# A two-layer convolution kernel: widening in float32, four buffers of node values in place of three, and group sums from one pair matrix and the identity

## The chip, the core and the metric

The kernel runs on one core of one Trainium2 chip. The metric is the device time in microseconds (us) of one execution. A core has five engines that run side by side and meet through semaphores: TensorE (PE in the profile; its weight loads are PEld), VectorE (DVE), ScalarE (ACT), GpSimd (POOL) and SyncE (SP), which here only starts transfers. TensorE writes to PSUM, eight banks of 2 KB in each of 128 partitions.

## The reference

```
x: (32, 64, 112, 112) float32
layer 0:  x = x + conv3x3(groupnorm32(x), sign(w) * alpha)          # 64 -> 64 channels
layer 1:  n = groupnorm32(x)
          h = w_in @ n                                              # 64 -> 256 channels
          h = irfft2(rfft2(8x8 patches of h) * fft_filt)
          h = depthwise conv3x3(h, w_dw)
          g = gelu(h[:128]) * h[128:]
          x = x + w_out @ g                                         # 128 -> 64 channels
```

groupnorm32 has 32 groups, so a group is two neighbouring channels.

## The kernel before

Two batch images lie on the 128 partitions (2 x 64 channels); there are 16 such pairs, which the code calls images n, and each is cut into 14 strips of 8 rows. A strip is 14 patches of 8x8 pixels, or 7 blocks of two patches; the blocks are worked in four groups, 0 to 2 of two blocks (512 columns of PSUM, 256 channels each) and 3 of one block (256 columns).

A strip of layer 1 goes through: normalising (ScalarE, L456), transposition to pixels on partitions (TensorE, L921), the copy xT (ScalarE, L464), the forward transform into an orthonormal basis of the patch's frequencies (TensorE, L930), and its copy xf (ScalarE, L469), which lies in the same memory as xT. xf is then split into two float16 halves, xf_hi (ScalarE, L478) and xf_lo (GpSimd, L351). *Widening* (`widened`, TensorE, L941) multiplies with w_in, split likewise into win_hi and win_lo: four products of halves, accumulated in PSUM, for each block and each of the two batch images. VectorE multiplies with the filter (`filtered`, hf, L690). *Evaluation* (`evaluated`, TensorE, L953, float32) takes the values of the patch at 121 nodes of a Toom-Cook scheme; VectorE multiplies them with the depthwise taps at the nodes (`weighted`, v32, L697). The products are split again: v_hi (ScalarE, L487) and v_lo (GpSimd, `low_nodes`, L357). *Interpolation* (`interpolated`, TensorE, L971) gives the 10x10 extended patches; then come gelu (ScalarE), the gate g (VectorE, L722), carries between strips (L706, L713, L511, L516), the projection with w_out (TensorE, L985) and the residual (GpSimd, L364).

The order of the work is written out by hand for every engine, step by step. In step t the front (transposition and transform) works on strip t, `mid` (widening, evaluation, v) on strip t-1, `up` (interpolation, gate) on strip t-2 and `done` (projection, residual) on strip t-3. Each image has 14 steps. Layer 0 of the *next* image runs in between: its statistics in steps 0 to 4, its group sums in step 5, and in steps 6 to 12 two convolution strips each (L912); the group sums of the next layer 1 stand in step 13. I call steps 6 to 12 convolution steps and the others plain; their orders differ. The last image has plain steps only.

PSUM banks 0-1 (P) and 2-3 (Q) are used in turn by widening, evaluation, transposition, transform and convolution. v32 has three buffers; the table V_BUF says which group of which image goes where, and VectorE waits, before each `weighted`, until GpSimd has read the buffer's last content (semaphores pool_vlo). In a plain step the order of v products is image 0: groups 3, 2, 1, 0; image 1: groups 3, 0, 1, 2. GpSimd's order in a plain step is v_lo of (0,3), residual, v_lo of (0,2), (0,1), (0,0), (1,3), then xf_lo, then v_lo of (1,0), (1,1), (1,2), residual.

Group sums (`groups`, L887 and L888): a pair matrix with 0.5 in 2x2 blocks gives the group's mean and mean variance, and a matrix c_apart = identity - pair gives each channel's distance from the group mean, whose square VectorE adds to the variance.

Of the kernel before, what the change touches and what calls it, by code (L numbers as in the profile page):

```python
# [10 lines left out]
P = 8  # L11
C = 64
# [59 lines left out]
def shape_constants():  # L72
# [18 lines left out]
    return {"forward": np.concatenate([basis, basis]), "pick": pick, "pair": pair, "apart": np.eye(HC) - pair, "identity": np.eye(HC),  # L91
# [3 lines left out]
def build(nc, x, conv_w, alpha, w_in, w_dw, filt, w_out, forward, pick, pair, apart, identity, nodes, taps, ext, out):  # L95
# [37 lines left out]
    with ctx:  # L133
# [8 lines left out]
        c_apart = sb("c_apart", [128, 128])  # L142
# [4 lines left out]
        win_hi = sb("win_hi", [128, C2], F16)  # L147
        win_lo = sb("win_lo", [128, C2], F16)
# [12 lines left out]
        xf_hi = sb("xf_hi", [128, NBLK, BPX], F16)  # L161
        xf_lo = sb("xf_lo", [128, NBLK, BPX], F16)
        hf = sb("hf", [BPX, IMGS, NBLK, C2])
        v32 = sb("v32", [128, 3, 2, 2, C2])
# [23 lines left out]
        win_sb = v32[:, 2, 0, 0, :]  # L188
# [39 lines left out]
        pool_xl = sem("pool_xl")  # L228
        act_xh = sem("act_xh")
# [18 lines left out]
        N_CONST = 15  # L248
# [34 lines left out]
        def _(sp):  # L283
# [10 lines left out]
            for dst, src in ((c_fwd[:], forward), (c_pick, pick), (c_pair[:], pair), (c_apart[:], apart), (c_id[:], identity),  # L294
                             (c_nodes[:], nodes), (c_taps, taps), (ext32, ext), (filt_sb, filt), (wdw_sb, w_dw),
                             (wout_sb[:], w_out), (win_sb[0:C], w_in), (win_sb[C:128], w_in)):
                sp.dma_start(dst, src).then_inc(dma_const, 16)
# [31 lines left out]
        def _(pool):  # L329
# [19 lines left out]
            def spectrum_low(n, s):  # L349
                pool.wait_ge(act_xh, n * STRIPS + s + 1)  # L350
                nc.gpsimd.tensor_tensor(xf_lo[:], xf[:], xf_hi[:], ALU.subtract).then_inc(pool_xl, 1)  # L351

            def low_nodes(b, s, img, grp):
# [3 lines left out]
                nc.gpsimd.tensor_tensor(v_lo[:, img, :, k0:k1, :], v32[:, V_BUF[kind(b, s)][img][grp], :, 0:k1 - k0, :],  # L357
# [9 lines left out]
            def image(n, par, prev, front, more):  # L367
                for t in range(STRIPS if front else OUT):
                    mid = item(n, t, MID, prev, front)
                    done = item(n, t, OUT, prev, front)  # L370
                    if more and CONV_FROM <= t <= CONV_TO:
# [14 lines left out]
                        if front:  # L386
                            spectrum_low(n, t)
# [5 lines left out]
                    else:  # L393
# [15 lines left out]
                        if front:  # L409
                            spectrum_low(n, t)  # L410
# [20 lines left out]
        def _(act):  # L431
# [41 lines left out]
            def spectrum_high(n, s):  # L473
# [781 lines left out]
```

## Time and profile before

| | |
|---|---|
| time, median of 3 runs | 5405.63 us (5405.21 to 5406.29) |
| profiled execution | 5406.3 us, span 5404.5 us |
| PE busy | 5202.6 us (96%) |
| PEld busy | 3195.1 us (59%) |
| DVE busy | 4642.3 us (86%) |
| ACT busy | 3739.5 us (69%) |
| POOL busy | 4643.1 us (86%) |
| granted TensorE clock | 0.996 of full speed |

The span is the time from the first to the last event of the profiled execution. Busy is the time in which an engine has at least one instruction under way; matmuls overlap each other, so the time from one start to the next says more of TensorE's pace than the length of one. L numbers are lines of the kernel before. A float32 matmul stands in the trace as two instructions.

### The profile page before, as it was taken

To read this page: it belongs to the slowest core of one execution; us is meant where nothing else is said; L and a number is where in the kernel's file an instruction comes from. 1 tells how busy PE (TensorE), PEld (TensorE's weight loads), DVE (VectorE), ACT (ScalarE), POOL (GpSimd) and SP (SyncE) were. 2 spreads that over 40 slices of the span, in tenths; PEclk is the share of its full clock that TensorE was granted. 3 is DMA by queue.
4 is the path that set the end of the run, shared out by engine and by line. 5 is a ranking of instruction groups with operands and counts; after the bars stand their busy time and mean duration, and the time that the engine had idled before them with its cause. 6 is when DMAs were issued, how large, how long until landed. Compare 5 with 4: busy or idle time off the path is not lost.

```text
span 5404.5 us, 201429 instructions
## 1 busy us (share of the span) xinstructions
PE 5202.6 (96%) x88868; PEld 3195.1 (59%) x88868; DVE 4642.3 (86%) x5703; ACT 3739.5 (69%) x4866; POOL 4643.1 (86%) x2727
## 2 busy tenths in 40 slices
PE   5999999999999999999999999999999999999998
PEld 4565655656556565565656556565665655656554
DVE  6889888888888888888898888988889888888876
ACT  3766767677676766767767676676766767677675
POOL 3889889898888988889888898888989889898898
PEclk9999999999999999999999999999999999999999
DMA  2011110110101111010010101101011110110000
GB/s 103 19 50 42 38 44 29 53 40 37 54 22 50 40 40 53 19 57 36 36 53 32 48 33 39 54 36 43 33 50 40 40 42 31 50 43 20 23 26 26
DMA packets 43953, 219.31 MB, mean 41 GB/s; under 512 B 5366, under 2 KB 6104, under 8 KB 36952
## 3 DMA queue, kind: packets, MB, share of 16 engines
q1 hardware_dynamic: 43096, 206.42, 9.9%
q8 instruction: 716, 11.73, 0.9%
q14 instruction: 141, 1.16, 0.1%
HBM read 103.64 MB, written 102.76 MB: 38 GB/s over the span
## 4 chain that ended last, share of the span: by engine, by line
PE 69%; DVE 15%; POOL 7%; issue 5%; ACT 3%; DMA 0%; DVEq 0%; SPq 0%; POOLq 0%; ACTq 0%
PE PS L953 20%; PE PS L971 17%; PE PS L912 14%; PE PS L941 10%; POOL v_lo L357 6%; DVE v L697 5%; PE PS L985 5%; DVE hf L690 4%; DVE g L722 2%; PE PS L921 2%; ACT v_hi L487 2%; DVE bn L628 2%; DVE PS L713 1%; ACT carry L516 1%; POOL xf_lo L351 0%
## 5 line engine op out<-in xcount | busy, mean ns | idle before, releaser
L357 POOL TENSOR_TENSOR v_lo<-v,v_hi 128x1024 f16<-128x1024 f32 (+1 forms) x1792 | 3354.6, 1898 | 455.4 <-ACT v_hi L487 455.0
L697 DVE TENSOR_TENSOR v<-PS,smul 128x1024 f32<-128x1024 f32 (+1 forms) x1792 | 1910.4, 1086 | 361.6 <-POOL v_lo L357 200.9
L487 ACT ACTIVATE v_hi<-v 128x1024 f16<-128x1024 f32 (+1 forms) x1792 | 1646.8, 944 | 717.5 <-DVE v L697 561.9
L953 PE MATMUL PS<-hf,c_nodes 64*64 64x512 f32 (+1 forms) x14336 | 1659.7, 556 | 70.4 <-DVE v L697 57.0
L971 PEld LDWEIGHTS PS<-c_ext,v_hi 128*128 128x128 f16 x14336 | 1129.9, 97 | 507.2 <-ACT carry L511 165.0
L971 PE MATMUL PS<-c_ext,v_hi 128*128 128x100 f16 (+2 forms) x14336 | 1258.9, 203 | 9.7 <-issue 4.1
L971 PE MATMUL PS<-c_ext,v_lo 128*128 128x100 f16 (+2 forms) x14336 | 1250.6, 202 | 0.0
L971 PEld LDWEIGHTS PS<-c_ext,v_lo 128*128 128x128 f16 x14336 | 1118.2, 97 | 1.2
L690 DVE TENSOR_TENSOR hf<-PS,mult 128x1024 f32<-128x1024 f32 (+1 forms) x896 | 954.8, 1086 | 86.7 <-PE PS L941 66.2
L953 PEld LDWEIGHTS PS<-hf,c_nodes 64*64 64x64 f32 x14336 | 406.8, 131 | 623.1 <-DVE v L697 219.7
L912 PE MATMUL PS<-S_hi,csign 64*64 64x448 f16 (+2 forms) x8640 | 746.8, 336 | 9.4 <-POOL S_lo L346 9.4
L912 PE MATMUL PS<-S_lo,csign 64*64 64x448 f16 (+2 forms) x8640 | 748.0, 337 | 0.0
L464 ACT ACTIVATE xT<-PS 128x896 f32<-128x896 f32 x224 | 205.6, 918 | 638.9 <-PE PS L921 638.9
L722 DVE TENSOR_TENSOR g<-PS,gel 128x912 f32<-128x912 f32 (+1 forms) x448 | 496.3, 1108 | 58.7 <-DVE PS L713 2.0
L346 POOL TENSOR_TENSOR S_lo<-n,S_hi 128x896 f16<-128x896 f32 x224 | 411.0, 1835 | 150.7 <-ACT S_hi L448 150.7
L351 POOL TENSOR_TENSOR xf_lo<-xT,xf_hi 128x896 f16<-128x896 f32 x224 | 425.5, 1900 | 83.4 <-ACT xf_hi L478 83.4
L941 PE MATMUL PS<-win_hi,xf_hi 64*128 64x256 f16 x3136 | 435.8, 274 | 59.0 <-DVE hf L690 33.1
L507 ACT ACTIVATE gel<-PS 128x912 f32<-128x912 f32 (+1 forms) x448 | 413.5, 923 | 110.1 <-DVE PS L706 109.0
L985 PE MATMUL PS<-g,wout_sb 128*64 128x448 f32 (+2 forms) x1792 | 445.6, 574 | 4.0 <-DVE g L722 2.3
L941 PE MATMUL PS<-win_hi,xf_lo 64*128 64x256 f16 x3136 | 429.1, 270 | 0.0
L941 PE MATMUL PS<-win_lo,xf_hi 64*128 64x256 f16 x3136 | 429.1, 270 | 0.0
L941 PE MATMUL PS<-win_lo,xf_lo 64*128 64x256 f16 x3136 | 429.0, 269 | 0.0
(74 smaller groups left out, 5846.0 us busy)
## 6 DMA issues: line engine op xcount, KB each, us to landing
out_x<-Xa SPq DMA_DIRECT2D x96, 448.0 KB, 2.5
out_x<-Xb SPq DMA_DIRECT2D x96, 448.0 KB, 2.5
Xa<-in_x SPq DMA_DIRECT2D x8, 2240.0 KB, 9.0
Xb<-in_x SPq DMA_DIRECT2D x8, 2240.0 KB, 8.9
Xa<-in_x SPq DMA_DIRECT2D x8, 1792.0 KB, 7.7
Xb<-in_x SPq DMA_DIRECT2D x8, 1792.0 KB, 6.8
Xa<-in_x SPq DMA_DIRECT2D x8, 1344.0 KB, 5.9
Xb<-in_x SPq DMA_DIRECT2D x8, 1344.0 KB, 6.7
```

Source lines behind the costliest of these rows:

```text
L351: nc.gpsimd.tensor_tensor(xf_lo[:], xf[:], xf_hi[:], ALU.subtract).then_inc(pool_xl, 1)
L357: nc.gpsimd.tensor_tensor(v_lo[:, img, :, k0:k1, :], v32[:, V_BUF[kind(b, s)][img][grp], :, 0:k1 - k0, :], v_hi[:, img, :, k0:k1, :], ALU. ...
L487: nc.scalar.activation(v_hi[:, img, :, k0:k1, :], v32[:, V_BUF[kind(b, s)][img][grp], :, 0:k1 - k0, :], ACT.Copy).then_inc(act_vhi[img], 1)
L507: nc.scalar.activation(gel[:, :, r0:r1, :], Y[:, :, r0:r1, :], ACT.Gelu).then_inc(act_y0, 1)
L690: nc.vector.tensor_tensor(hf[:, :, k0:k1, :], PS[:, bank:bank + 2, 0:(k1 - k0) * C2].rearrange("p i (k c) -> p i k c", c=C2), mult[:].unsq ...
L697: nc.vector.tensor_tensor(v32[:, V_BUF[kind(b, s)][img][grp], :, 0:k1 - k0, :], PS[:, bank:bank + 2, 0:(k1 - k0) * C2].rearrange("p i (k c ...
L722: nc.vector.tensor_tensor(g[:, img, r0:r1, :].rearrange("p r (b c) -> p b r c", c=YC), Y[:, :, r0:r1, :], gel[:, :, r0:r1, :], ALU.mult).t ...
L912: last = nc.tensor.matmul(PS[c * C:(c + 1) * C, bank + h, i0 * W:(i0 + m) * W], csign[r * C:(r + 1) * C, tap, :], S[r * C:(r + 1) * C, row ...
L941: last = nc.tensor.matmul(PS[:, bank + r, (k - k0) * C2:(k - k0 + 1) * C2], xf[r * C:(r + 1) * C, k, :], win[r * C:(r + 1) * C, :], start= ...
L953: last = nc.tensor.matmul(PS[points, bank + side, 0:(k1 - k0) * C2], c_nodes[half, points], hf[half, img, k0:k1, :].rearrange("p k c -> p ...
L971: last = nc.tensor.matmul(Y[:, b0, :, col - b0 * YC:end - b0 * YC], v[:, img, patch % 2, patch // 2, half * HC:(half + 1) * HC], c_ext[:, ...
L985: last = nc.tensor.matmul(Z[img * C:(img + 1) * C, 0:(r1 - r0) * HALF_W], wout_sb[:], g[:, img, r0:r1, 1 + q * HALF_W:1 + (q + 1) * HALF_W ...
```

## The change

Widening is done in float32: TensorE takes xf and w_in as they are, in four matmuls a block, one for each 64x64 tile (batch image r, side of the block), and nothing is accumulated. xf_hi, xf_lo, win_hi, win_lo and the instructions that made them go; w_in gets memory of its own. ScalarE's copy of the next pixels into xT, which waited for GpSimd's xf_lo, waits for the last widening of the strip before. v32 gets a fourth buffer, and a product's buffer is its place in the order of its image; V_BUF goes. The product at place k of image 1 waits for GpSimd's v_lo at place k of image 0 of the same strip, and that of image 0 for image 1's of the strip before. The pair matrix is passed with its sign turned, c_apart goes, and its product is made by two accumulated matmuls, identity and then pair; three signs in VectorE's small operations follow.

```diff
-    return {"forward": ..., "pair": pair, "apart": np.eye(HC) - pair, "identity": np.eye(HC),
+    return {"forward": ..., "pair": -pair, "identity": np.eye(HC),
...
-    V_BUF = {"plain": [{3: 0, 2: 1, 1: 2, 0: 0}, {3: 1, 0: 2, 1: 0, 2: 1}],
-             "conv": [{3: 0, 0: 1, 1: 2, 2: 0}, {3: 1, 2: 2, 1: 0, 0: 1}]}
...
-        v32 = sb("v32", [128, 3, 2, 2, C2])
+        v32 = sb("v32", [128, 4, 2, 2, C2])
...
 # ScalarE: pixels
                 if n or s:
-                    act.wait_ge(pool_xl, n * STRIPS + s)
+                    act.wait_ge(pe_hf, 4 * (n * STRIPS + s))
...
 # ScalarE: spectrum_high and GpSimd: spectrum_low, in every step
-                nc.scalar.activation(xf_hi[:], xf[:], ACT.Copy).then_inc(act_xh, 1)
-                nc.gpsimd.tensor_tensor(xf_lo[:], xf[:], xf_hi[:], ALU.subtract).then_inc(pool_xl, 1)
...
 # VectorE, plain step (before = not the very first strip)
                         if mid:
-                            if before and conv_before:
-                                dve.wait_ge(pool_vlo[1], 4 * i - 1)
-                            elif before:
-                                dve.wait_ge(pool_vlo[1], 4 * i - 1)
+                            if before:
+                                dve.wait_ge(pool_vlo[1], 4 * i - 3)
                             weighted(b, s, 0, 3, BANK_P)
...
                         if mid:
-                            dve.wait_ge(pool_vlo[0], 4 * i + 2)
+                            dve.wait_ge(pool_vlo[0], 4 * i + 1)
                             weighted(b, s, 1, 3, BANK_Q)
...
                         if mid:
-                            dve.wait_ge(pool_vlo[0], 4 * i + 3)
+                            dve.wait_ge(pool_vlo[0], 4 * i + 2)
                             weighted(b, s, 1, 0, BANK_Q)
...
 # TensorE
-                return nc.tensor.matmul(Z[:, 2:3], c_apart[:], channels[:, 0:1], start=True, stop=True)
+                nc.tensor.matmul(Z[:, 2:3], c_id[:], channels[:, 0:1], start=True, stop=False)
+                return nc.tensor.matmul(Z[:, 2:3], c_pair[:], channels[:, 0:1], start=False, stop=True)
...
             def widened(b, s, grp, bank):
-                pe.wait_ge(pool_xl, b * STRIPS + s + 1)
+                pe.wait_ge(act_xf, b * STRIPS + s + 1)
                 for k in range(k0, k1):
-                    for part, (xf, win) in enumerate(((xf_hi, win_hi), (xf_lo, win_hi), (xf_hi, win_lo), (xf_lo, win_lo))):
-                        for r in range(IMGS):
-                            last = nc.tensor.matmul(PS[:, bank + r, (k - k0) * C2:(k - k0 + 1) * C2],
-                                                    xf[r * C:(r + 1) * C, k, :], win[r * C:(r + 1) * C, :],
-                                                    start=part == 0, stop=part == 3)
+                    for r, side in ((0, 0), (1, 1), (0, 1), (1, 0)):
+                        last = nc.tensor.matmul(PS[side * P * P:(side + 1) * P * P, bank + r, (k - k0) * C2:(k - k0 + 1) * C2],
+                                                xf[r * C:(r + 1) * C, k, side * P * P:(side + 1) * P * P],
+                                                win_sb[r * C:(r + 1) * C, :], start=True, stop=True)
                 last.then_inc(pe_hf, 1)
```

The order on TensorE in step 5 of the first image, before: the end of one widening call, the group sums (L887, L888) and the start of the next call.

```order
L941 MATMUL PS<-win_hi,xf_hi 128x256 x2
L941 MATMUL PS<-win_hi,xf_lo 128x256 x2
L941 MATMUL PS<-win_lo,xf_hi 128x256 x2
L941 MATMUL PS<-win_lo,xf_lo 128x256 x2
L887 MATMUL PS<-mvx,c_pair 128x2
L888 MATMUL PS<-mvx,c_apart 128x1
L941 MATMUL PS<-win_hi,xf_hi 128x256 x2
```

The same place after (here three widening calls of 20 matmuls read as one row, and each tile has 64 rows):

```order
L931 MATMUL PS<-c_ext,v_hi 128x10x10
L901 MATMUL PS<-win_sb,xT 64x256 x20
L847 MATMUL PS<-mvx,c_pair 128x2
L848 MATMUL PS<-mvx,c_id 128x1
L849 MATMUL PS<-mvx,c_pair 128x1
L901 MATMUL PS<-win_sb,xT 64x256 x8
L931 MATMUL PS<-c_ext,v_hi 128x10x10
```

A block has four matmul calls in place of eight, and the group sums three in place of two; no call has moved past another.

The order on GpSimd in a plain step of the first image, before (Xa is the residual, v_lo in 128x2x256 is group 3):

```order
L357 TENSOR_TENSOR v_lo<-v,v_hi 128x2x256
L364 TENSOR_TENSOR Xa<-g,Xa 128x8x56
L357 TENSOR_TENSOR v_lo<-v,v_hi 128x2x512 x3
L357 TENSOR_TENSOR v_lo<-v,v_hi 128x2x256
L351 TENSOR_TENSOR xf_lo<-xT,xf_hi 128x896
L357 TENSOR_TENSOR v_lo<-v,v_hi 128x2x512 x3
```

And after:

```order
L343 TENSOR_TENSOR v_lo<-v,v_hi 128x2x256
L350 TENSOR_TENSOR Xa<-g,Xa 128x8x56
L343 TENSOR_TENSOR v_lo<-v,v_hi 128x2x512 x3
L343 TENSOR_TENSOR v_lo<-v,v_hi 128x2x256
L343 TENSOR_TENSOR v_lo<-v,v_hi 128x2x512 x3
```

Only xf_lo is gone from between the products of image 1. VectorE's order of operations is the same as before in every step; only the numbers it waits for have changed.

## Rows read from the trace of the kernel before

**Rows 1.** Windows: us; busy PE, PEld, DVE, ACT, POOL; clock; DMA. Statistics, convolution, plain.
```profile
2154.66:2175.45 20.79, 19.73 (x322) 11.70 (x320) 19.24 (x25) 14.72 (x20) 18.75 (x12) 1.00 0.06 21
...
2226.52:2253.08 26.56, 26.45 (x477) 16.52 (x476) 22.77 (x28) 18.72 (x24) 22.73 (x14) 1.00 0.05 19
...
5241.90:5262.48 20.58, 19.66 (x322) 11.71 (x320) 16.20 (x19) 14.86 (x20) 18.80 (x12) 1.00 0.07 25
```

**Rows 2.** Timeline, TensorE: start, us, instruction; convolution step, then plain step.
```profile
2228.70 0.66 PE L953 MATMUL PS<-hf,c_nodes 64*64 64x256 f32 x8
2229.18 0.99 PE L930 MATMUL PS<-c_fwd,xT 64*64 64x64 f32 x56
2230.25 1.09 PE L953 MATMUL PS<-hf,c_nodes 64*64 64x512 f32 x8
...
5184.56 0.66 PE L953 MATMUL PS<-hf,c_nodes 64*64 64x256 f32 x8
...
5186.57 1.09 PE L953 MATMUL PS<-hf,c_nodes 64*64 64x512 f32 x8 [0.54 <-DVE v L697]
```

**Rows 3.** Timeline, VectorE: the same convolution step and plain step.
```profile
2229.50 0.69 DVE L697 TENSOR_TENSOR v<-PS,smul 128x512 f32<-128x512 f32 x1 [0.29 <-PE PS L953]
...
5185.82 0.69 DVE L697 TENSOR_TENSOR v<-PS,smul 128x512 f32<-128x512 f32 x1 [0.76 <-POOL v_lo L357]
```

**Rows 4.** Timeline, GpSimd: the same plain step.
```profile
5183.64 7.47 POOL L357 TENSOR_TENSOR v_lo<-v,v_hi 128x1024 f16<-128x1024 f32 x4 [1.43 <-ACT v_hi L487]
5191.08 1.90 POOL L351 TENSOR_TENSOR xf_lo<-xT,xf_hi 128x896 f16<-128x896 f32 x1
```

**Rows 5.** Waits of the span: who for whom, us in total, times, longest.
```profile
DVE v L697 <- POOL v_lo L357: 200.9, 328, 1.4
...
PE PS L953 <- DVE v L697: 57.0, 107, 1.8
```

**Rows 6.** Chain of waits at the start: start, us, what.
```profile
37.27 0.43 DVE win_lo L865
...
110.81 0.96 ACT xf_hi L478
...
111.83 1.89 POOL xf_lo L351
```

**Rows 7.** Timeline, TensorE: widening calls in the plain step.
```profile
5193.61 0.27 PE L941 MATMUL PS<-win_hi,xf_hi 64*128 64x256 f16 x2
...
5194.57 0.28 PE L941 MATMUL PS<-win_hi,xf_hi 64*128 64x256 f16 x2
...
5196.00 0.28 PE L941 MATMUL PS<-win_hi,xf_hi 64*128 64x256 f16 x2 [0.38 <-DVE hf L690]
```

**Rows 8.** Timeline, TensorE: another convolution step.
```profile
2004.86 1.09 PE L953 MATMUL PS<-hf,c_nodes 64*64 64x512 f32 x8
2005.88 0.22 PE L971 MATMUL PS<-c_ext,v_hi 128*128 128x100 f16 x1
...
2007.37 1.95 PE L953 MATMUL PS<-hf,c_nodes 64*64 64x512 f32 x16
2009.25 0.99 PE L985 MATMUL PS<-g,wout_sb 128*64 128x448 f32 x4
2010.21 0.28 PE L941 MATMUL PS<-win_hi,xf_hi 64*128 64x256 f16 x2
...
2011.19 0.22 PE L971 MATMUL PS<-c_ext,v_hi 128*128 128x100 f16 x1
```

**Rows 9.** Line L930 over the span: duration min/median/max in ns.
```profile
L930 PEld LDWEIGHTS PS<-c_fwd,xT x12544: 129/135/228, 108.0 to 5350.9; 64*64 64x64 f32 x200
L930 PE MATMUL PS<-c_fwd,xT x12544: 216/218/366, 108.0 to 5351.0; 64*64 64x64 f32 x200
```

**Rows 10.** Timeline, TensorE: group sums in step 5.
```profile
2190.82 0.38 PE L887 MATMUL PS<-mvx,c_pair 128*128 128x2 f32 x2
2191.07 0.36 PE L888 MATMUL PS<-mvx,c_apart 128*128 128x1 f32 x2
```

More of the change, by code:

```diff
@@ L90, in shape_constants, with build @@
     pair = np.kron(np.eye(HC // 2), np.full((2, 2), 0.5))
-    return {"forward": np.concatenate([basis, basis]), "pick": pick, "pair": pair, "apart": np.eye(HC) - pair, "identity": np.eye(HC),
+    return {"forward": np.concatenate([basis, basis]), "pick": pick, "pair": -pair, "identity": np.eye(HC),
             "nodes": np.concatenate([nodes, nodes]), "taps": taps, "ext": ext}
-def build(nc, x, conv_w, alpha, w_in, w_dw, filt, w_out, forward, pick, pair, apart, identity, nodes, taps, ext, out):
+def build(nc, x, conv_w, alpha, w_in, w_dw, filt, w_out, forward, pick, pair, identity, nodes, taps, ext, out):
     B, _, H, W = x.shape
@@ L293, in _ @@
                 sp.dma_start(alpha_sb[r * C:(r + 1) * C], alpha).then_inc(dma_conv, 16)
-            for dst, src in ((c_fwd[:], forward), (c_pick, pick), (c_pair[:], pair), (c_apart[:], apart), (c_id[:], identity),
+            for dst, src in ((c_fwd[:], forward), (c_pick, pick), (c_pair[:], pair), (c_id[:], identity),
                              (c_nodes[:], nodes), (c_taps, taps), (ext32, ext), (filt_sb, filt), (wdw_sb, w_dw),
-                             (wout_sb[:], w_out), (win_sb[0:C], w_in), (win_sb[C:128], w_in)):
+                             (wout_sb[:], w_out), (win_sb[0:C, :], w_in), (win_sb[C:128, :], w_in)):
                 sp.dma_start(dst, src).then_inc(dma_const, 16)
@@ L356, in low_nodes @@
                 pool.wait_ge(act_vhi[img], 4 * (b * STRIPS + s) + at + 1)
-                nc.gpsimd.tensor_tensor(v_lo[:, img, :, k0:k1, :], v32[:, V_BUF[kind(b, s)][img][grp], :, 0:k1 - k0, :],
+                nc.gpsimd.tensor_tensor(v_lo[:, img, :, k0:k1, :], v32[:, V_ORDER[kind(b, s)][img].index(grp), :, 0:k1 - k0, :],
                                         v_hi[:, img, :, k0:k1, :], ALU.subtract).then_inc(pool_vlo[img], 1)
@@ L486, in high_nodes @@
                     act.wait_ge(pe_y, 4 * i - 2 + 2 * img)
[L487 removed]
+                nc.scalar.activation(v_hi[:, img, :, k0:k1, :], v32[:, V_ORDER[kind(b, s)][img].index(grp), :, 0:k1 - k0, :],
                                      ACT.Copy).then_inc(act_vhi[img], 1)
@@ L697, in weighted @@
                 nc.vector.tensor_tensor(
-                    v32[:, V_BUF[kind(b, s)][img][grp], :, 0:k1 - k0, :],
+                    v32[:, V_ORDER[kind(b, s)][img].index(grp), :, 0:k1 - k0, :],
                     PS[:, bank:bank + 2, 0:(k1 - k0) * C2].rearrange("p i (k c) -> p i k c", c=C2),
@@ L762, in image @@
                         if mid:
-                            dve.wait_ge(pool_vlo[0], 4 * i + 1)
+                            if before:
+                                dve.wait_ge(pool_vlo[1], 4 * i)
                             weighted(b, s, 0, 2, BANK_P)
@@ L806, in image @@
                         if mid:
[L807 to L810 removed]
+                            if before:
+                                dve.wait_ge(pool_vlo[1], 4 * i - 3)
                             weighted(b, s, 0, 3, BANK_P)
[L812 to L815 removed]
+                            if before:
+                                dve.wait_ge(pool_vlo[1], 4 * i - 2)
                             weighted(b, s, 0, 2, BANK_Q)
@@ L821, in image @@
                         if mid:
-                            if before and conv_before:
-                                dve.wait_ge(pool_vlo[1], 4 * i - 2)
-                            elif before:
-                                dve.wait_ge(pool_vlo[1], 4 * i - 2)
+                            if before:
+                                dve.wait_ge(pool_vlo[1], 4 * i - 1)
                             weighted(b, s, 0, 1, BANK_Q)
-                            dve.wait_ge(pool_vlo[0], 4 * i + 1)
+                            if before:
+                                dve.wait_ge(pool_vlo[1], 4 * i)
                             weighted(b, s, 0, 0, BANK_P)
```

72 lines of the change are left out of this document (18 added, 54 removed).

## The prediction

> **What bounds the kernel now.** The busy shares of the whole span come first, but three engines are above 80% there, and that does not say which of them ends a wait. So I cut the span at the starts of successive strip transposes and read the windows [rows 1]. The reader is to see that there are only two kinds of step. A step with convolutions takes 26.56 us of which TensorE is busy 26.45: nothing but TensorE's own time counts there. A plain step takes about 20.6 us with 19.66 on TensorE, 16.2 on VectorE (19.24 where it also takes statistics) and 18.8 on GpSimd. There are 7 convolution steps in each of 15 images, 105, and 7 x 15 + 14 = 119 plain ones.
>
> Next I looked for the missing 0.9 us of a plain step, in the timelines. With x2 or x8 in a row several instructions are merged. TensorE evaluates the 256-wide group of the second image (E3), runs the forward transform (F), and then must wait with the next evaluation until VectorE has emptied the bank of E3. From E3 to that next evaluation the plain step takes 5186.57 - 5184.56 = 2.01 us, the convolution step 2230.25 - 2228.70 = 1.55 [rows 2]. On VectorE the reason is plain: its v product starts 5185.82 - 5184.56 = 1.26 us after E3 in the plain step, released by GpSimd's v_lo, and 0.80 us after E3 in the convolution step, released by TensorE [rows 3]. v32 has three buffers, and GpSimd holds the one wanted. GpSimd works from 5183.64 without a pause: four v_lo (7.47 us), then xf_lo (1.90 us) before the v_lo of the next groups [rows 4]. Over the span TensorE idles 57.0 us in 107 places for a v product, while VectorE waits 200.9 us in 328 places for v_lo, most of it with no consequence [rows 5].
>
> **The v32 buffers.** With four buffers, buffer = place in the order, the product of (image 1, group 3) waits for v_lo of (image 0, group 3) in place of that of (image 0, group 2). The former is done by 5182.2, where GpSimd begins to idle 1.43 us, the latter, the first of the four, by 5185.8 [rows 3, 4]. So the product is free to go as soon as E3 has ended and VectorE is idle. E3 ends at 5185.22 (start 5184.56, took 0.66) and VectorE is free from 5185.82 - 0.76 = 5185.06 [rows 2, 3]: start near 5185.3, as in the convolution step. The later products wait for one v_lo less in the same way. Nothing new is queued behind them. TensorE gets back, in each of the 107 places, 57.0 / 107 = 0.53 us less the 0.07 that stays even in the convolution step (F runs 2229.18 + 0.99 = 2230.17, the evaluation starts at 2230.25 [rows 2]). That is 57.0 - 107 x 0.07 = 49.5. One place, the longest (1.8 us), lies in the tail, where GpSimd's chain ends last anyway: 48 us back. Bounds: nothing, if another wait stands behind it; 57 if all goes.
>
> What is late next in a plain step with statistics is VectorE: 19.24 busy [rows 1] plus some 20 hand-overs. Its statistics sit right behind the waiting product and move up with it, so it starts its own long stretch some 0.5 earlier, and the gain should survive. Below it lies TensorE's 19.66.
>
> **The halves of the spectrum go.** ScalarE loses xf_hi (0.96 us a step) and GpSimd xf_lo (1.90) [rows 4, 6]. Each is hidden already in the steady state: widening is a step later. I price them at nothing there, beside giving GpSimd 1.9 us of slack a step, with which v_lo of the last groups comes 1.9 earlier. They are on the chain only in the first image, where TensorE waits for xf_hi 0.96 and xf_lo 1.89 before its first widening, and then in its second step again for xf_lo [rows 6]: the first 0.96 + 1.89 = 2.9 us, and of the 1.9 of the second I take 1.5, since TensorE still has an interpolation to end: 4.4 us gained. ScalarE's wait for the pixels moves from xf_lo to the last widening of the step before; TensorE issues all four widenings ahead of the transposes that ScalarE waits for anyway, so it is free.
>
> **The widening itself.** Before: for each of 7 blocks, 8 float16 matmuls of 256 columns, two at a time (the two row halves). After: 8 instructions of float32 on four 64x64 tiles at a time (each float32 matmul is two instructions: F has 56 [rows 2] where the code makes 7 x 4). A two-block call before takes 0.96 to the next call (5193.61 to 5194.57) and 0.98 to an interpolation (2010.21 to 2011.19); a block's 8 rows are some 0.44 [rows 7, 8]. For float32 the same shape is in the trace: E3 is one block of 256 columns. From its start to F is 0.48 (2228.70 to 2229.18 [rows 2]). A 512-column evaluation: two of them and the gap to the next line are 2009.25 - 2007.37 = 1.88 us, 0.43 for each round of four beyond the first and about 0.05 once at a call's start [rows 8]. So 256 columns take 0.215 a round, two rounds a block, 0.43: the same as before. A two-block call is 0.05 + 4 x 0.215 = 0.91 against 0.96, before an interpolation 1.02 (2004.86 to 2005.88) against 0.98, the one-block call 0.48 against 0.44 [rows 2, 7, 8].
>
> That rounds with a new stationary side each time run that fast is shown by F: 56 instructions, 14 rounds, in 0.99 - 0.22 = 0.77 for 13 intervals, 0.059 a round of 64 columns, with 8 weight loads a block [rows 2, 9]. The Trainium skill (TensorE: Matmul & The Clock Gate, The mechanism) says that a weight load overlaps running matmuls only when its row group differs. By that rule each round of four, which occupies both row groups, would bare its load; F's 0.059 a round, with loads of 135 ns each [rows 9], disagrees, so I keep it as the basis of a rival below.
>
> In a plain step the second-last widening call is followed by a wait for VectorE (5194.57 to 5196.00, 1.43 us [rows 7]), which swallows the 0.05 saved in the two-block calls, while the 0.04 of the one-block call and 0.04 of the last call move the chain of hf products: +0.07 a step, 119 x 0.07 = 8.3 us. In a convolution step the call before the interpolation costs 0.04 more, and the next three, which VectorE's hf products pace, -0.01 and +0.03 (the longer last round, before whose end VectorE may not start): +0.06, 105 x 0.06 = 6.3 us. Bounds from the same rows: if each of the three two-block calls saves its 0.05 and nothing swallows it, 224 x 0.15 = -34 us; if each of the four calls costs 0.04 more with no cover, 224 x 0.16 = +36 us.
>
> **Group sums.** One matmul more, two instructions, in 2 x 16 places. In the step of the statistics they stand between widening calls; the first line takes 0.25 (2190.82 to 2191.07 [rows 10]), and the new one adds as much. The two that stand there now fill the wait for VectorE (1.43 us after the call's start, less its own 0.96, leaves 0.47 [rows 7]), so little covers the third: 0.2 x 30 = 6 us, and nothing for the two before the first strip. The sign folded into the matrix changes no instruction's size. The two casts of w_in leave VectorE at the start (0.43 us on the chain for one [rows 6], 0.6 for both), and one 64 KB load of a constant goes: 0.6 us.
>
> **Sum.** -48 - 4.4 - 0.6 + 8.3 + 6.3 + 6 = -32.4 us. The execution profiled took 5406.3 us (span 5404.5 and 1.8 around it), 0.7 above the median of 5405.63. 5406.3 - 32.4 = 5373.9; from the median it would be 5373.2. I say 5374.
>
> **Rivals.**
> First, slower. The float32 rounds do not hide their weight loads. Place: every widening, 14 rounds a step of which 4 open a call. Price: the 0.05 us that a call's first round already pays, for the other 10: 0.5 us x 224 = 112 us, so 5374 + 112 less some cover in the plain steps, about 5475. It decides from 32.4 / 224 = 0.14 us a step, 14 ns for each of the 10 rounds. For it: a stationary side that is data with 256 moving columns stands nowhere in the trace. Against: F. The skill's rule above would give this result.
> Second, the gain meets a new wait. In the steps with statistics (3 of 7 plain ones, 45 in all, with the 0.47 wait) VectorE, at 19.24 of 20.79 us [rows 1], has no room and holds the step: 45 x 0.47 = 21 us less gain, 5395. For it: that share. Against: its stretch starts when the product does.
> Third, more is gained. GpSimd's slack and ScalarE's 0.95 us also loosen hand-overs that I count as fixed (the 0.07 at each of the 107 places, 7.5 us), and the widening's 14.6 are covered: 5374 - 7.5 - 14.6 = 5352.
> That the change does nothing of what it says (the wait only changes its name, 5400) I hold for nearly excluded, since the convolution step shows the place without the GpSimd wait.
>
> **Chances.** Forecast 0.72 (5364 to 5386), slower rival 0.06, statistics 0.12, more gained 0.10. A measurement of this kernel tells 0.2%, 11 us, from no change; faster than 5394.8 is the forecast, the third rival and a third of the second with it, 0.86; the same 0.08; slower 0.06. The range that holds 8 in 10 runs from 5356 to 5393: the low end some way to the third rival, the high end nearly to the second and to half of the +36 of the widening.
>
> **What would show it.** Plain steps of about 20.2 us in place of 20.6, convolution steps at 26.6; TensorE's wait for v products from 57 to below 12 us; VectorE's wait for v_lo near zero; GpSimd near 78% busy (18.8 - 1.9 in a plain step); a two-block widening call at 0.91 us, its rounds 0.215 apart. Wrong would be rounds of 0.26 or more, convolution steps of 27 us or more (first rival), or statistics steps that stay at 20.7 while the last image's fall (second).

## The result and the profile after

| | time, median | ratio to before, 95% interval |
|---|---|---|
| before, 20 runs | 5405.1 us | |
| changed, 20 runs | 5396.25 us (5393.1 to 5398.88) | 0.9983 [0.9977, 0.9990] |

The change saves 8.9 us, 0.17%, and the interval lies clear of 1. 5374 was forecast, with 5356 to 5393 as the range, so the gain is about a quarter of the 32 us forecast.

First the page of the changed kernel: the span, then the busy time of each engine.

```profile
span 5394.6 us, 200882 instructions
PE 5249.1 (97%) x88932; PEld 3061.1 (57%) x88932; DVE 4631.7 (86%) x5701; ACT 3526.7 (65%) x4642; POOL 4236.2 (79%) x2503
```

GpSimd is at 79% (78% was expected) and ScalarE lost 4 points. But TensorE has 46.5 us *more* busy time than before (5202.6). Next the windows from one strip transpose to the next, in the order of [rows 1]: a step with statistics, a convolution step, a plain step of the last image, and, fourth, step 13.

```profile
2148.28:2168.58 20.30, 19.89 (x322) 11.08 (x320) 19.31 (x25) 13.77 (x19) 16.91 (x11) 1.00 0.05 21
2219.23:2245.95 26.72, 26.61 (x477) 15.89 (x475) 22.68 (x28) 17.76 (x23) 20.74 (x13) 1.00 0.05 20
5235.13:5255.38 20.25, 19.84 (x322) 11.07 (x320) 16.25 (x19) 13.91 (x19) 16.94 (x11) 1.00 0.06 24
...
2399.07:2419.70 20.63, 19.94 (x321) 11.08 (x319) 19.84 (x24) 13.92 (x19) 16.84 (x11) 1.00 0.07 25
```

The statistics step fell from 20.79 to 20.30 and the plain one from 20.58 to 20.25; the convolution step rose from 26.56 to 26.72. The medians over images 1 to 14, from the starts of the transposes, in us:

| step | 0 | 1 | 2 | 3 | 4 | 5 | 6 to 11 each | 12 | 13 | sum |
|---|---|---|---|---|---|---|---|---|---|---|
| before | 20.70 | 20.39 | 20.16 | 20.79 | 20.66 | 30.41 | 26.56 | 18.10 | 20.70 | 331.3 |
| after | 20.30 | 20.53 | 20.05 | 20.30 | 20.60 | 30.05 | 26.72 | 18.49 | 20.62 | 331.3 |

A row of the table runs from the transpose of that step to the next, so the group sums of steps 5 and 13 fall into columns 4 and 12. The fourteen middle images gain nothing. What is gained lies in the first image (328.6 to 323.2), the last one (267.5 to 264.1 for 13 steps) and the tail. The steps without convolutions are also less alike than the prediction's two kinds had them: in the kernel before, TensorE's wait for a v product is 0.5 to 0.6 us in steps 0, 3, 4, 5 and 13, 0.27 in step 2, and none in step 1.

The waits (engine, line, released by: us in total, times, longest) say that the wait in question is gone, and which one grew:

```profile
DVE v L670 <- POOL v_lo L343: 5.5, 17, 0.6
PE PS L913 <- DVE v L670: 4.5, 12, 0.9
...
PEld PS L901 <- DVE hf L663: 160.5, 312, 0.8
DVE hf L663 <- PE PS L901: 101.0, 322, 3.9
```

Against [rows 5], VectorE's wait for v_lo fell from 200.9 us to 5.5 and TensorE's for a v product from 57.0 to 4.5. In their place the two engines wait for each other at widening. Before, these two rows were:

```profile
PEld PS L941 <- DVE hf L690: 103.9, 296, 0.7
...
DVE hf L690 <- PE PS L941: 66.2, 185, 6.7
```

TensorE in the plain step shows both. E3, F and the next evaluation, which answer to [rows 2]:

```profile
5199.00 0.66 PE L913 MATMUL PS<-hf,c_nodes 64*64 64x256 f32 x8
5199.48 0.99 PE L891 MATMUL PS<-c_fwd,xT 64*64 64x64 f32 x56
5200.55 1.09 PE L913 MATMUL PS<-hf,c_nodes 64*64 64x512 f32 x8
```

5200.55 - 5199.00 = 1.55 us where it was 2.01. And widening, which answers to [rows 7] (the first row is three calls merged, the second the last call):

```profile
5207.14 2.57 PE L901 MATMUL PS<-win_sb,xT 64*64 64x256 f32 x40
5210.05 1.09 PE L901 MATMUL PS<-win_sb,xT 64*64 64x256 f32 x16 [0.34 <-DVE hf L663]
5211.07 0.22 PE L931 MATMUL PS<-c_ext,v_hi 128*128 128x100 f16 x1
```

From the first call to the last are 2.91 us, before 5216.59 - 5213.76 = 2.83 in the last image; the last call takes 1.02 to the interpolation, before 0.98.

### The profile page after: what moved, and what is told of

Its sections match the earlier page's. It is cut to its first block, busy times and chain, and to the rows that moved or that the text cites. A ratio compares the mean times of both kernels' runs of the same rounds, so it can differ in the third digit from the quotient of the medians.

```text
span 5394.6 us, 200882 instructions
## 1 busy us (share of the span) xinstructions
PE 5249.1 (97%) x88932; PEld 3061.1 (57%) x88932; DVE 4631.7 (86%) x5701; ACT 3526.7 (65%) x4642; POOL 4236.2 (79%) x2503
## 2 busy tenths in 40 slices
DMA packets 43804, 219.20 MB, mean 41 GB/s; under 512 B 5350, under 2 KB 5960, under 8 KB 36808
## 4 chain that ended last, share of the span: by engine, by line
PE 86%; DVE 10%; issue 3%; DMA 0%; ACT 0%; POOL 0%; DVEq 0%; SPq 0%; POOLq 0%; ACTq 0%
PE PS L913 28%; PE PS L931 21%; PE PS L873 14%; PE PS L901 12%; PE PS L945 7%; DVE v L670 5%; PE PS L882 4%; DVE hf L663 3%; DVE bn L601 1%; DVE g L695 1%; DVE PS L679 0%; DVE PS L686 0%; DMA alpha_sb<-in_alpha 0%; POOL v_lo L343 0%; PE PS L847 0%
## 5 line engine op out<-in xcount | busy, mean ns | idle before, releaser
L901 PE MATMUL PS<-win_sb,xT 64*64 64x256 f32 x12544 | 824.9, 388 | 48.0 <-DVE hf L663 28.9
L901 PEld LDWEIGHTS PS<-win_sb,xT 64*64 64x64 f32 x12544 | 413.7, 132 | 394.3 <-DVE hf L663 160.5
L945 PE MATMUL PS<-g,wout_sb 128*64 128x448 f32 (+2 forms) x1792 | 445.6, 574 | 7.7 <-DVE g L695 5.9
L873 PEld LDWEIGHTS PS<-S_hi,csign 64*64 64x64 f16 x8640 | 314.1, 107 | 142.8 <-DVE v L670 28.5
L873 PEld LDWEIGHTS PS<-S_lo,csign 64*64 64x64 f16 x8640 | 314.6, 106 | 135.2 <-issue 32.1
L469 ACT ACTIVATE g<-PS 128x448 f32<-128x448 f32 (+1 forms) x448 | 244.7, 546 | 81.3 <-PE PS L945 79.3
```

The source lines that it names most:

```text
L873: last = nc.tensor.matmul(PS[c * C:(c + 1) * C, bank + h, i0 * W:(i0 + m) * W], csign[r * C:(r + 1) * C, tap, :], S[r * C:(r + 1) * C, row ...
L901: last = nc.tensor.matmul(PS[side * P * P:(side + 1) * P * P, bank + r, (k - k0) * C2:(k - k0 + 1) * C2], xf[r * C:(r + 1) * C, k, side * ...
L945: last = nc.tensor.matmul(Z[img * C:(img + 1) * C, 0:(r1 - r0) * HALF_W], wout_sb[:], g[:, img, r0:r1, 1 + q * HALF_W:1 + (q + 1) * HALF_W ...
```

## The experiments

Ratios are to the kernel before, run beside each. "Plain" is a step of the last image, "conv" a convolution step, before 20.57 and 26.56.

The forecasts name their theories by a letter. A and B are one pair in experiments 1 and 4, and others in 2 and in 3.

### 1 to 4: one part at a time

**1.** Before, with four places for node values. To fit, one is of half size and xf_lo lies over xf; widening stays in float16.

```diff
-        xf_lo = sb("xf_lo", [128, NBLK, BPX], F16)
+        xf_lo = xT[...].bitcast(F16)...
+        v3 = sb("v3", [128, 2, 1, C2])
-                    act.wait_ge(pool_xl, n * STRIPS + s)
+                    act.wait_ge(pe_hf, 4 * (n * STRIPS + s))
```

> The kernel before with a fourth v32 buffer alone (the place of group 3, always first, is half as wide, and xf_lo lies in the memory of xT, so that it fits; ScalarE's next pixels then wait for the last widening). Widening stays in float16, group sums as before. Theory A (the buffers give all that was predicted, and the loss lies in the float32 widening and the group sums): the wait for the v product after the forward transform falls from 1.53 to 1.06 us in plain steps, 46 us less in all, about 5359. Theory B (the buffers' gain is itself given back in a later wait, whatever the widening): 5385 to 5400.

5397.08 us, 0.9984 [0.9976, 0.9993]; plain 20.52, conv 26.56. That is theory B. The wait for the buffer is gone, and most of the gain with it. The waits of this kernel (L933 is widening, xT now also holds xf_lo, L945 evaluation) and a piece of its chain:

```profile
PE PS L933 <- POOL xT L353: 50.6, 81, 4.0
...
PE PS L945 <- DVE v L699: 5.3, 12, 0.9
```
```profile
5200.15 7.47 POOL v_lo L359 x4
5207.62 1.86 POOL xT L353
5209.48 0.14 issue
5209.62 0.63 PE PS L933 x8
```

GpSimd's order did not move when TensorE came earlier: four v_lo, then xf_lo, and widening now stands waiting for it. In step 3 of the middle images the evaluation behind F starts 0.56 us earlier than before, the first widening only 0.06. In the kernel before, xf_lo ended at 5191.08 + 1.90 = 5192.98 [rows 4], and the first widening of that step stands here:

```profile
5193.17 0.28 PE L941 MATMUL PS<-win_hi,xf_hi 64*128 64x256 f16 x2
```

It was early by 0.19 us, and the chain above has 0.14 from the end of xf_lo to the widening that waited for it, so that some 0.05 was to spare. In steps 2 and 5 of the middle images it was 0.15 already before the change: nothing to spare. The 50.6 us of this wait must not be set against the 51.7 won for v products: 22.0 of them lie in step 5, which keeps its length (30.42) and where the kernel before waited too, 1.24 us a time under the name of a v product, and 8.3 in the first image. The plain steps proper hold 20.

**2.** Before, with widening in float32 alone (three buffers, old group sums).

> The kernel before with the float32 widening alone (no xf_hi, xf_lo, win_hi, win_lo), three v32 buffers, old group sums. Theory A (each of the four widening calls of a step costs TensorE 0.04 more, since its first weight load stands bare behind a semaphore wait and a float32 load is longer): 224 x 0.15 = +34, less 4.4 at the start, about 5435. Theory B (the widening is as cheap as forecast, +10): 5415. The v product's wait stays at 1.53 us in plain steps in both, since it hangs on v_lo of the same strip that stands ahead of xf_lo in GpSimd's order.

5434.41 us, 1.0049 [1.0035, 1.0063]; plain 20.72, conv 26.72. The time is theory A's; its cause is not, as experiments 7 to 11 show. A convolution step costs 0.16 us more (0.06 was forecast), a plain step of the last image 0.14 (0.07 was forecast). In the middle images the medians of steps 0, 2, 3, 5 and 13 rise by 0.06 to 0.10 only, of step 1 by 0.13 and of step 4 by 0.19. The wait for the buffer stays.

**3.** Before, with the new group sums alone.

> The kernel before with the new group sums alone (pair matrix and identity, one matmul more, in 30 places of the loop). Theory A: 0.22 us of TensorE each, +6 to +7, about 5412. Theory B (covered by the wait for VectorE's product): within 1 us of before.

5415.18 us, 1.0018 [1.0009, 1.0027]; 5412 was forecast by theory A, and B is out. The two steps with group sums take 0.23 us more. In the changed kernel:

```profile
2183.61 0.38 PE L847 MATMUL PS<-mvx,c_pair 128*128 128x2 f32 x2
2183.86 0.36 PE L848 MATMUL PS<-mvx,c_id 128*128 128x1 f32 x2
2184.08 0.36 PE L849 MATMUL PS<-mvx,c_pair 128*128 128x1 f32 x2
2184.37 1.09 PE L901 MATMUL PS<-win_sb,xT 64*64 64x256 f32 x16
```

**4.** Parts 1 and 3 together: the changed kernel but for the float32.

> The changed kernel with the widening put back into float16 halves (four v32 buffers and the new group sums stay; xf_lo in the memory of xT). Theory A: e1 plus the group sums, 5359 + 7 = 5366, that is 30 below the changed kernel. Theory B (something other than the widening eats the gain): above 5385.

5403.74 us, 0.9998 [0.9989, 1.0007]. Theory B holds, and the changed kernel is 7.5 us faster than this one: float32 costs TensorE time, but gives back a little more by taking xf_lo off GpSimd.

### 5 and 6: the same buffers with xf_lo earlier

```diff
                             low_nodes(mid[0], mid[1], 0, 0)
-                            low_nodes(mid[0], mid[1], 1, 3)
                         if front:
                             spectrum_low(n, t)
                         if mid:
+                            low_nodes(mid[0], mid[1], 1, 3)
                             low_nodes(mid[0], mid[1], 1, 0)
```

> The kernel before, widening in float16, with the four places for node values of the first experiment (one of half size, xf_lo written over xf), and one thing moved: in a step without convolution GpSimd makes xf_lo ahead of the low half of image 0's last group, v_lo(1,3), not behind it. Theory C: the gain of the four places is real (0.41 us a plain step from transform to evaluation) and was taken back in the first experiment because xf_lo came 0.41 us late for widening; made some 1.16 us earlier it is no longer late, and a plain step is 20.57 - 0.41 = 20.1 to 20.2 us in place of 20.52: 119 x 0.41 = 49 less than before, 5355 to 5362 us, and the first weights of widening wait for VectorE's hf again. Rival D (the buffers alone are worth no more than 8 us in any order, the waits lie elsewhere, or v_lo(1,3), now 1.9 us later, holds image 1): over 5385 us.

5372.71 us, 0.9939 [0.9927, 0.9952], 33 us less than before. Windows of steps 3 and 5 and of the plain step:

```profile
2142.34:2162.57 20.23, 19.73 (x321) 11.71 (x319) 19.31 (x25) 14.71 (x20) 18.75 (x12) 1.00 0.06 23
2182.77:2213.40 30.63, 28.98 (x482) 17.21 (x480) 24.40 (x29) 23.72 (x31) 29.70 (x19) 1.00 0.08 32
...
5192.69:5212.80 20.11, 19.66 (x322) 11.73 (x320) 16.26 (x19) 14.87 (x20) 18.75 (x12) 1.00 0.06 24
```

Theory C stands: the plain step is 20.11, 0.46 less, and step 3, with statistics, fell by 0.56. The memory is laid out as in experiment 1, so that it was the order and not the layout that ate the gain there. C's 5355 to 5362 was too low: it counted 0.41 in all 119 steps. Step 1 (20.39) had no wait for a v product and gains nothing, step 2 gains 0.27, and there are two places more. Step 5 rose from 30.41 to 30.61: GpSimd is busy 29.70 of it, and the chain there is GpSimd alone up to the convolution (L904):

```profile
2194.76 3.22 POOL v_lo L359 x2
2197.98 1.79 POOL S_lo L348
2199.77 4.21 POOL v_lo L359 x2
2203.98 1.79 POOL S_lo L348
2205.77 1.02 POOL Xa L366
2206.80 1.12 POOL v_lo L359
2207.91 1.80 POOL S_lo L348
...
2209.84 3.62 PE PS L904 x72
```

The changed kernel, without xf_lo, runs that step in 30.05. The other place is step 13 (20.56), below.

**6.** The same with fewer waits and the distance from the group mean made by VectorE:

```diff
-                nc.tensor.matmul(Z[:, 2:3], c_id[:], channels[:, 0:1], ...)
-                return nc.tensor.matmul(Z[:, 2:3], c_pair[:], channels[:, 0:1], ...)
+                nc.vector.tensor_tensor(groupx[:, 2:3], mvx[:, 0:1], Z[:, 0:1], ALU.add)
```

> As the kernel with xf_lo made earlier, and three things more: the wait for xf_lo stands at the first widening call of a step alone, the second call's implied wait for VectorE is gone, and a group's distance from its mean is made by VectorE from the mean of the pair matrix (no identity product). If a wait at the head of a call costs its bare first load some 0.01 us in float16, 1 to 3 us less than that kernel; group sums as before or 3 us less. Theory C: 5350 to 5362. Theory D: over 5385.

5371.09 us, 0.9937 [0.9924, 0.9949], within 2 us of the fifth, where 5350 to 5362 was forecast. The column with the group sums of layer 0 fell from 20.19 to 20.11; the plain step did not move, and step 5 rose from 30.61 to 30.70.

### 7 to 11: why float32 costs 0.15 us a step

My theory was that each wait at the head of a call bares the first float32 weight load. In the changed kernel most calls do start with 0.267 us from the first to the second round of four, against 0.216 later.

```diff
# 7
-                pe.wait_ge(act_xf, b * STRIPS + s + 1)
                 for k in range(k0, k1):
+                    pe.wait_ge(act_xf, b * STRIPS + s + 1)
# 8
-                pe.wait_ge(act_xf, b * STRIPS + s + 1)
+                if first:
+                    pe.wait_ge(act_xf, b * STRIPS + s + 1)
```

> The changed kernel with one thing added: the wait for xf, long met, stands ahead of each block of a widening call and not ahead of the call alone (3 more waits a step, 672 in all). Theory (the first weight load behind a wait lies bare, in float32 0.05 us of it): 672 x 0.05 = 34 us slower, 5430. Rival (a met wait costs nothing; the four calls are longer by their streams or by the gap to what follows): 5396, within 3 us.

> The changed kernel with the wait for xf at the first widening call of a step alone, and without the implied wait for VectorE ahead of the second call of a step without convolution; calls two to four keep a wait for VectorE wherever their bank has a reader before them. Theory (a wait bares the first float32 load): only a call left with no wait gains, one of four in plain steps, 119 x 0.05 = 6 us, 5390 us. Rival: 5396, within 3 us.

With more waits 5395.07 us, 0.9982 [0.9973, 0.9991]; with fewer 5401.75, 0.9993 [0.9984, 1.0002]. The theory falls: 672 waits more cost nothing, and with fewer nothing is won. The round behind an added wait stays at 0.216 us, where a bared load would have made it 0.267; in both kernels plain is 20.25, conv 26.72 and each call as long as in the changed kernel. The eighth is 5.5 us above the changed kernel, though the intervals of the two ratios overlap (0.9984 to 1.0002 and 0.9977 to 0.9990). Its profile shows single steps that are 0.3 us or more over their median, 11.1 us in the middle images against 5.7; why, stays open.

The next theory (L) looked at who waits for the end of a call. The times from the start of one call to the next in a plain step of the last image, in us, up to the interpolation and the evaluation behind it:

| widening | 1st to 2nd | 2nd to 3rd | 3rd to 4th | 4th to interpolation | interpolation | sum over before |
|---|---|---|---|---|---|---|
| before | 0.447 | 0.955 | 1.431 | 0.980 | 1.390 | |
| all in float32 | 0.483 | 0.994 | 1.432 | 1.027 | 1.415 | +0.15 |
| 9: first | 0.595 | 0.885 | 1.486 | 0.980 | 1.390 | +0.13 |
| 10: second, third | 0.540 | 0.914 | 1.530 | 0.980 | 1.389 | +0.15 |
| 11: last | 0.447 | 0.954 | 1.431 | 1.027 | 1.415 | +0.07 |

The edit, in the kernel of the third experiment (xf_hi and xf_lo are still made):

```diff
+                    if whole:
+                        for r, side in ((0, 0), (1, 1), (0, 1), (1, 0)):
+                            last = nc.tensor.matmul(PS[side * 64:..., bank + r, ...], xf[...], win_sb[...], ...)
+                        continue
```

> The kernel of the third experiment (before, with the new group sums: plain step 20.57 us, convolution step 26.56, F to the next evaluation 1.53) with the first widening call of every step in float32 and the other three in float16; xf_lo is still made and still waited for. Theory L (a call is dearer only where something waits for its end: the last float32 matmul and the load behind a wait that ends late are longer, a wait already met costs nothing): VectorE's first hf starts 0.08 us later after the call, and the third call, which waits for it, too: plain step +0.08, 20.65; convolution step +0.05, 26.61; 119 x 0.08 + 105 x 0.05 = 15 us over the third experiment, ratio 1.0045. Theory P (each float32 call costs the same 0.04 us, wherever it stands): +0.04 in both, 9 us.

> The same with the second and third call in float32 and the first and last in float16. Theory L: in a plain step VectorE works through hf without a gap while they run, so nothing waits for their ends: plain step +0.00 to +0.02, 20.57 to 20.59; in a convolution step they stand back to back in front of the last, +0.05. 5 to 8 us over the third experiment. Theory P: +0.08 in both, 18 us.

> The same with the last call alone in float32. Theory L: its end and its hf stand on the way to the interpolation and the evaluation behind it: plain step +0.07, 20.64; convolution step +0.05, 26.61; 14 us over the third experiment. Theory P: +0.04 in both, 9 us.

5426.22, 5427.50 and 5427.98 us; 1.0036 [1.0022, 1.0050], 1.0039 [1.0026, 1.0052], 1.0037 [1.0023, 1.0050]. Their windows (9, 10, 11; conv, then plain):

```profile
2288.13:2314.74 26.61, 26.51 (x479) 16.34 (x475) 22.77 (x28) 18.75 (x24) 22.48 (x14) 1.00 0.05 20
5242.52:5263.23 20.71, 19.73 (x322) 11.53 (x320) 16.26 (x19) 14.88 (x20) 18.81 (x12) 1.00 0.07 25
```
```profile
2286.53:2313.17 26.64, 26.54 (x479) 16.27 (x476) 22.77 (x28) 18.76 (x24) 22.46 (x14) 1.00 0.05 20
5242.11:5262.84 20.73, 19.70 (x321) 11.26 (x320) 16.30 (x19) 14.88 (x20) 18.81 (x12) 1.00 0.07 25
```
```profile
2291.43:2318.05 26.62, 26.51 (x479) 16.34 (x475) 22.77 (x28) 18.75 (x24) 22.47 (x14) 1.00 0.05 19
5245.70:5266.35 20.65, 19.73 (x321) 11.53 (x320) 16.20 (x19) 14.88 (x20) 18.80 (x12) 1.00 0.06 25
```

The times don't tell the theories apart: the three lie 11 to 13 us over the third experiment, and each ratio's interval is some 7 us to either side. The steps do, in part.

In the plain step the last call behaves as L says: +0.08, made of 0.047 in the call and 0.025 in the interpolation behind it, whose evaluation waits for the call's hf; P's 0.04 is out for it. The second and third call fit neither: L had 20.57 to 20.59, P 20.65, and the step takes 20.73. Where the second call's format differs from the first one's, it starts later (0.595 for 0.483, 0.540 for 0.447), which neither theory had, and the three kernels alone cost 0.35 in a plain step where all calls together cost 0.15.

Where the remaining 0.075 arises with all calls in float32, the chain behind the first call shows. VectorE's first hf and the weight load of the third call, which waits for it, in the changed kernel (first call at 5207.14) and then in the kernel before (first call at 5213.76):

```profile
5207.87 0.69 DVE L663 TENSOR_TENSOR hf<-PS,mult 128x512 f32<-128x512 f32 x1 [0.91 <-PE PS L901]
5208.61 0.64 PEld L901 LDWEIGHTS PS<-win_sb,xT 64*64 64x64 f32 x16 [0.41 <-DVE hf L663]
```
```profile
5214.41 0.69 DVE L690 TENSOR_TENSOR hf<-PS,mult 128x512 f32<-128x512 f32 x1 [0.84 <-PE PS L941]
5215.15 0.10 PEld L941 LDWEIGHTS PS<-win_hi,xf_hi 64*128 64x128 f16 x2 [0.20 <-DVE hf L690]
```

VectorE starts 0.73 us behind the first call, before 0.65, and the third call 1.477 behind it in place of 1.402; from there to the fourth call nothing changes (1.432 and 1.431). The length of the second call does not come into it.

The convolution step has the same chain, behind its second call, the one of one block. Medians over the middle images in us, from the start of each call to the start of what follows:

| widening, convolution step | 1st to interpolation | 2nd to 3rd | 3rd to 4th | 4th to projection |
|---|---|---|---|---|
| before | 0.979 | 0.447 | 0.955 | 0.977 |
| all in float32 | 1.027 | 0.482 | 0.994 | 1.024 |

The first call costs 0.048 more, the last 0.047, and between the second and the fourth, which waits for the second one's hf, lie 1.476 in place of 1.402: 0.17 together, 0.16 in the step. One at a time the steps of 9, 10 and 11 rise by 0.04, 0.07 and 0.06 over the third experiment's, where L had 0.05 for each and P 0.04, 0.08 and 0.04.

### 12 to 14: step 13, and the best version

In step 13 VectorE makes nb, one column, beside GpSimd's v_lo (GpSimd and VectorE of the changed kernel):

```profile
2402.54 4.24 POOL L343 TENSOR_TENSOR v_lo<-v,v_hi 128x1024 f16<-128x1024 f32 x2 [1.44 <-ACT v_hi L462]
```
```profile
2404.26 0.69 DVE L670 TENSOR_TENSOR v<-PS,smul 128x512 f32<-128x512 f32 x1 [0.29 <-PE PS L913]
2404.87 1.93 DVE L636 SCALAR_TENSOR_TENSOR nb<-group,rstd 128x1 f32<-128x1 f32 x1
```

nb starts at 2404.87 and ends at 2406.80, v_lo at 2406.78. In all 15 places of this kernel's profile nb ends 0.015 to 0.021 us behind a v_lo, and in those of the kernel before 0.015 to 0.019; the median length was 1.47 there and is 1.93 now, which is what the buffers won at its start. In the start-up, beside an idle GpSimd, nb takes 0.16 us. nb reads two operands from SBUF, the core's memory in which the tiles lie. The Trainium skill (SBUF — State Buffer, section "SBUF: two separate sides") says that a VectorE operation with two SBUF inputs and a GpSimd operation that reads SBUF exclude each other for the whole instruction; the trace agrees, with 1.93 us for one column.

```diff
                 nc.gpsimd.tensor_tensor(rstd1[:], ve1[:], m_half[:], ALU.pow).then_inc(pool_rstd1, 1)
+                pool.wait_ge(pool_rstd1, n + 1)
+                nc.gpsimd.tensor_tensor(nb1[:], group1[:, 0:1], rstd1[:], ALU.mult).then_inc(pool_nb1, 1)
...
-                            shift_1(n + 1)
```

> The changed kernel with the two products nb = group mean times rstd (128x1) made by GpSimd right behind rstd, and not by VectorE. Theory H (in step 13 VectorE's nb is held until GpSimd's pair of v_lo ends: it ended 0.02 us behind it both before and after, 1.46 and 1.93 us long, so that the 0.47 us won by the buffers are lost there again and v(1,0) comes as late as before): step 13 20.62 to 20.29 us, 15 x 0.33 = 5 us less, 5391. Rival (nb is long by itself, or something else holds v(1,0)): no change, 5396.

> The same, and the distance from the group's mean by VectorE from one product of the pair matrix, so that one float32 product stands between the widening calls where the changed kernel has three. If the group sums cost TensorE 0.22 us for each product beyond those that the kernel before had: 5391 less 30 x 0.22 = 6.6, and no more than 30 x 0.25 = 7.5 less for the second product, 5378 to 5385. Rival (VectorE's operation more takes it back): 5391.

> The kernel of the sixth experiment (float16 widening, four places for node values, xf_lo made earlier, distance from the mean by VectorE; 5371.1 us) with nb made by GpSimd. Theory H: step 13 20.56 to 20.23, 15 x 0.33 = 5 us less, 5366. Rival: 5371.

| | time | ratio to before |
|---|---|---|
| 12, changed kernel, nb by GpSimd | 5391.19 us | 0.9978 [0.9969, 0.9987] |
| 13, and distance from the mean by VectorE | 5382.44 us | 0.9961 [0.9949, 0.9974] |
| 14, kernel 6, nb by GpSimd | 5366.74 us | 0.9931 [0.9918, 0.9945] |

Step 13 of the twelfth:

```profile
2399.01:2419.31 20.30, 19.89 (x322) 11.08 (x320) 18.18 (x23) 13.91 (x19) 16.85 (x11) 1.00 0.07 25
```

Step 13 fell from 20.63 to 20.30, VectorE is busy 18.18 of it in place of 19.84, and all three times came out as theory H and the price of the group products had them. For nb alone it is the steps that show it, since the intervals of the ratios overlap (12 against the changed kernel, 14 against 6): step 13 falls from 20.62 to 20.30 in the twelfth and from 20.56 to 20.23 in the fourteenth, and no other step moves. The fourteenth is the best of all, 37 us below the kernel before, with widening still in float16.

## Why the prediction was wrong

The time missed by 22 us. The widening's price carried 15 of them, a VectorE operation that the sum did not have 5.

**Widening, +14.6. This step failed.** The stream was right: rounds of 0.216 us for 0.215 forecast, and the first rival is dead. What was mis-sized is the end of a call for VectorE, which waits for it. The sentence "the 0.04 of the one-block call and 0.04 of the last call move the chain of hf products" took for both what TensorE itself loses from start to start. VectorE loses more: behind the one-block call its hf starts 0.73 us after the call's start in place of 0.65, and the third call 0.07 later; behind the last call it is 0.047 and another 0.025 in the interpolation. So +0.07 in the plain step became +0.15.

In the convolution step +0.06 became +0.16. The first call's 0.04 was right (0.048). The next three, "which VectorE's hf products pace, -0.01 and +0.03", cost 0.07 and 0.047. The -0.01 came from "0.91 against 0.96", where the 0.96 is not the length of a float16 call: its two blocks stream in 0.87, and the weight load behind them waits for VectorE's hf (the second pair of rows in experiments 7 to 11). With float32 the same wait ends later, 0.99 after the call's start, and there was no 0.05 to save.

In steps 0, 2, 3 and 13 of the middle images the forecast +0.07 was right (0.06 to 0.08), in steps 1, 4 and 5 it was 0.10 to 0.19. Together that is 30 us by the medians of experiment 2's steps; by its time it is 29 with the 5 us in it that were to be gained at the start, so 34.

**The buffers, -48.** Right as a wait: TensorE's idle time for v products fell by 52.5 us, and [rows 3] named the cause. And right as a gain in the changed kernel: it is 38.2 us faster than experiment 2, from which it differs by the buffers and the group sums. With 7 for the group sums and the 5 that step 13 takes back that is 50, and by the medians of the steps 45. But there was a condition that the prediction missed, and it is in the next paragraph.

**The halves of the spectrum, priced at nothing.** The sum did not suffer by it, but the reason was false: "Each is hidden already in the steady state: widening is a step later". The strip that is widened is one behind, but xf_lo is made in the same step shortly ahead of widening, with 0.19 us between them of which 0.14 is the hand-over, and the term above moved TensorE 0.46 us forward. Experiment 1 has the one without the other: 8 us in place of 48. In the changed kernel the sum stays right, because float32 removes xf_lo; but then it is float32's gain as much as the buffers', and experiment 5 has most of it by moving one instruction.

**Group sums, +6.** Right: 30 x 0.23 = 7 by the steps, 9.7 (5 to 15) by experiment 3's ratio.

**Not in the sum at all:** step 13, where nb takes back 0.33 us of what the buffers win, 15 x 0.33 = 5 us (experiment 12).

**The second rival** had the right time (5395) by the wrong mechanism. The steps with statistics were not held: step 3 fell by 0.49, and by 0.56 in experiment 5, at 19.31 us of VectorE. Step 1 did not fall because it had no such wait to lose before.

By the medians of the steps, and with the two terms of the start as forecast, which no run measures by themselves, the sum is -45 - 4.4 - 0.6 + 30 + 7 + 5 = -8. The profiled execution fell from 5406.3 to 5396.35, by 10.

## What to carry to other kernels

A wait that is removed lets an engine come earlier only where all else it meets is made earlier too: before pricing it, look for each input of the next stages how long ahead of its use it ends, and by whose order. Compare two versions of a call from the start of the call to the start of what follows in both, and see first whether a wait lies in between. Price its end separately, since an engine that waits for a call waits for its last instruction, not for its rate. Look for tiny VectorE operations with two SBUF inputs beside GpSimd's long ones: here one of 0.16 us took 1.93, to the end of the GpSimd operation that it stood beside.

## What the runs showed of the hardware

- 672 semaphore waits that are long met, in front of matmuls, cost nothing that 11 runs can tell (experiment 7: 5395.07 us against 5396.25), and the round behind such a wait stays at 0.216.
- Four float32 64x64 tiles with data as the stationary side and 256 moving columns run at 0.216 us a round, weight loads of 133 ns hidden. The Trainium skill (TensorE: Matmul & The Clock Gate, The mechanism) says that a weight load overlaps running matmuls only when its row group differs, though a sentence above it also lets a load into the background weight buffer go ahead. By the first, each load of such a round would lie bare; the trace disagrees and has only the first round of most calls longer, 0.267.
- Such a float32 call streams as fast as the float16 call of the same work (0.432 and 0.436 us a block), but what follows it on TensorE starts 0.047 us later (1.027 for 0.980), and VectorE, where it waits for a call of one block, 0.08 (0.73 for 0.65).
- In a plain step the second widening call starts about 0.1 us later where its format differs from that of the first (0.595 for 0.483 and 0.540 for 0.447, experiments 9 and 10). In the convolution step of experiment 10 a float16 call behind a float32 one loses 0.002 (0.996 for 0.994), but there it stands behind a wait for VectorE. I had not looked for it, and no run takes it apart.
